# Twelve-sublayer decoder on one core: order of work at the starts, round changes and ends of four sublayers

## The reference, cut to what matters

```python
# layer 0, first attention: 16 heads of 8, a decay on the weights, causal; x += attn(ln(x))
# layer 0, cross-attention (mLSTM, 8 heads of 16), gates from tokens and context:
log_fg = log_sigmoid(f_pre); lf_cs = cumsum(log_fg)
log_d  = lf[t] - lf[s] + i_pre[s], -inf for s > t
m      = max over s of log_d;  d = exp(log_d - m)
out    = ((q k^T) * d) v / (max(|row sum|, exp(-m)) + eps)
# layer 2, first sublayer (Mamba): x_conv = silu(conv(x W_in) + b); B, C, dt from x_conv
h = exp(dt * A) * h + (dt * x_conv) * B;  y = sum over 16 states of h * C
y = (y + x_conv * D) * silu(z);  x += y W_out
# layer 3: a decayed attention over heads (alpha), then sigmoid(layernorm(x)) * wkv
# ("receptance"), then a two-expert MoE with 14 experts
```

## Time and profile before

| | |
|---|---|
| median of 3 runs | 1565.3 us (1560.38, 1565.3, 1567.12) |
| profiled execution | 1562.59 us; its span 1559.7 us, 28295 instructions |
| mean granted TensorE clock | 0.944 |
| mLSTM and MoE of layer 0 | about 157 to 300 us of the span |
| Mamba | about 706 to 977 us |
| layer 3 with the feed-forward ahead of it | about 1207 to 1557 us |

### The profile page before, as it was taken

One profiled execution on the slowest core, in us unless ns is written; L12 is line 12 of the kernel. 1 busy time (PEld: TensorE's weight loads), 2 busy tenths in 40 slices (PEclk: granted clock), 3 DMA queues, 4 the chain that ended last, 5 costly groups with the idle time before them and its releaser, 6 DMA issues. The chain is left out here.

```text
span 1559.7 us, 28295 instructions
## 1 busy us (share of the span) xinstructions
PE 1354.9 (87%) x9646; PEld 885.0 (57%) x9646; DVE 1179.8 (76%) x2532; ACT 879.3 (56%) x2677; POOL 773.8 (50%) x740
## 2 busy tenths in 40 slices
PE   6997887899789998898988988899998678877895
PEld 3554555555567775563333432788887434436784
DVE  7997567789777785465898998777776787887654
ACT  4774342377677773225777775577766244343663
POOL 5667353222655442414988889433336222454553
PEclk9998898999999999999999999999999798878997
DMA  7000000000000000002000000000000400001353
GB/s 312 1 2 1 1 1 1 1 2 2 1 1 2 2 2 0 1 1 97 1 1 1 0 1 1 1 2 1 2 2 6 137 1 1 1 1 53 107 162 99
DMA packets 38494, 39.48 MB, mean 25 GB/s; under 512 B 2128, under 2 KB 35536, under 8 KB 37584
## 3 DMA queue, kind: packets, MB, share of 16 engines
q1 hardware_dynamic: 36304, 33.48, 6.5%
q0 software_dynamic: 2048, 4.20, 0.9%
HBM read 23.52 MB, written 14.16 MB: 24 GB/s over the span
## 5 line engine op out<-in xcount | busy, mean ns | idle before, releaser
L837 POOL TENSOR_TENSOR l_xattn_probs<-l_xattn_probs,l_xattn_recip 128x512 f32<-128x512 f32 x128 | 133.1, 1040 | 220.1 <-DVE l_xattn_recip L776 219.8
L1055 ACT ACTIVATE l_attn_probs<-ps,l_attn_neg_max 128x128 f32<-128x128 f32 x512 | 145.2, 383 | 64.0 <-DVE l_attn_neg_max L1126 62.7
L2786 POOL TENSOR_TENSOR l_mamba_hc<-l_mamba_h,l_mamba_c 128x512 f32<-128x512 f32 x128 | 159.0, 1270 | 0.0
L2707 DVE TENSOR_TENSOR_SCAN l_mamba_h<-ps,l_mamba_dBx 128x512 f32<-128x512 f32 x128 | 152.7, 1213 | 1.8 <-ACT ps L2604 0.7
L2480 PE MATMUL ps<-l_mamba_hc,w_const 128*128 128x512 f32 x256 | 136.3, 638 | 19.2 <-POOL l_mamba_hc L2786 16.5
L771 DVE COPY l_xattn_probsT<-ps 128x512 f32<-128x512 f32 x128 | 88.0, 687 | 69.7 <-PE ps L623 69.7
L246 POOL TENSOR_TENSOR rs<-rs,neg_half 128x4 f32<-128x4 f32 (+1 forms) x32 | 43.4, 1357 | 151.8 <-DVE rs L240 151.7
L722 ACT ACTIVATE l_xattn_probs<-ps,l_xattn_neg_max 128x128 f32<-128x128 f32 x256 | 91.8, 388 | 41.3 <-DVE l_xattn_neg_max L766 41.3
L722 ACT ACTIVATE l_xattn_probs<-l_xattn_biased,l_xattn_neg_max 128x128 f32<-128x128 f32 x256 | 99.3, 391 | 12.2 <-DVE l_xattn_neg_max L766 12.2
L2604 ACT ACTIVATE ps<-l_mamba_th,l_mamba_w_a_bias,l_mamba_w_a_scale 128x508 f32<-128x508 f32 x128 | 97.1, 782 | 13.4 <-DVE l_mamba_h L2707 12.9
L2480 PEld LDWEIGHTS ps<-l_mamba_hc,w_const 128*128 128x128 f32 x256 | 44.8, 194 | 86.7 <-POOL l_mamba_hc L2786 69.3
(11 more groups left out here) (595 smaller groups left out, 3638.3 us busy)
## 6 DMA issues: line engine op xcount, KB each, us to landing
sorted_in<-l_nothing SPq DMA_DIRECT2D x4, 1344.0 KB, 11.5
sorted_out<-l_wide SPq DMA_DIRECT2D x8, 512.0 KB, 3.9
w_early<-in_l_moe SPq DMA_DIRECT2D x1, 3688.0 KB, 12.0
l_large<-sorted_in SPq DMA_DIRECT2D x4, 576.0 KB, 6.3
w_l_xattn<-in_l_xattn SPq DMA_DIRECT2D x1, 2176.0 KB, 18.7
l_large<-sorted_in SPq DMA_DIRECT2D x4, 512.0 KB, 4.4
w_early<-in_l_xattn SPq DMA_DIRECT2D x1, 1890.0 KB, 11.8
sorted_out<-l_wide SPq DMA_DIRECT2D x4, 320.0 KB, 2.6
```

The lines of the kernel that those rows point to most:

```text
L837: nc.gpsimd.tensor_tensor(probs[:, D % 2, n, :, :], probs[:, D % 2, n, :, :], along(recip[:, D % 2, n, :], [P, HALF, P]), ALU.mult).then_i ...
L1055: ins = nc.scalar.activation(probs[:, t % 4, g, :], S_of(t)[:, g * P:(g + 1) * P], ACT.Exp, bias=neg_max[:, t % 2, g:g + 1], accum_out=total)
L2707: nc.vector.tensor_tensor_scan(flat(h[:, t % 2, half, :, :]), G.ps[:, DA_BANK[half], :], flat(dBx[:, t % 2, half, :, :]), 0.0, ALU.mult, A ...
L2786: nc.gpsimd.tensor_tensor(heads4(hc[:, t % 4, half, :]), h[:, t % 2, half, :, :], c_sb[:, t % 3, :, :], ALU.mult).then_inc((hc0_set, hc1_s ...
```

## The change

1. `narrow_attention`, layer 0 only: POOL's `scales` moves from t = 30 to t = 32, behind the last L1182, and its `apply` of 12 blocks (2 per step) becomes 8 blocks after the loop.
2. mLSTM: the last ten instructions of `prepare` move out of the layernorm block to the head of DVE's list (`prepare_split`). The second half of `c_stats` moves behind the rows. ACT does tanh, exp and ln of the forget gate and then tanh of the input gate. `neg_m` is negated before `floor_row`. PE may spread `a_row` before `neg_m` is there, behind 6 instead of 14 `keep_clock` matmuls. POOL's second to fourth `q_pair` wait for the rows.
3. Mamba: `spread_c` goes between the two `add_state` of a step; `x_bc` is taken in halves (n = 10, 11); `x_step`, `steps`, `take_xd`, `tanh` and `step_size` come one to two places earlier; one `tangent_x` moves from n = 10 to n = 9 and DVE's `branch_x(0)` ahead of the second scan of n = 10. At the end DVE's `variances` goes ahead of `gated`, DVE applies 6 blocks, and PE gets 3 and 6 `keep_clock` matmuls.
4. Layer 3: `receptance(0)` goes behind the copy of round 3's tokens, `receptance(1)` ahead of `take_tokens(0)`, and `receive(1)` ahead of `subtract_top(3)`.

```diff
-                if t == DONE:
+                if t == (STEPS if projected else DONE):
                     ahead.scales(pool)
-                if t > DONE and ahead.applied < ahead.first:
+                if not projected and t > DONE and ahead.applied < ahead.first:
                     ahead.apply(pool, nc.gpsimd, 2)
+            if projected:
+                ahead.apply(pool, nc.gpsimd, 8)
...
             nc.vector.tensor_scalar(gain[:], w["gain"], 1.0, None, ALU.add)
+
+        def prepare_split(dve):
+            link = Link(dve, prepared, 2)
             for n in range(2):
...
             score(0)
-            pe.wait_ge(gates_set, 2)
-            keep_clock(14)
-            pe.wait_ge(rows_set, 1)
+            pe.wait_ge(gates_set, 1)
+            keep_clock(6)
             for n, row in enumerate((a_row, neg_m)):
+                if n == 0:
+                    pe.wait_ge(own, 2)
+                else:
+                    pe.wait_ge(rows_set, 1)
...
-            for n, gate in enumerate((gate_f, gate_i)):
-                act.wait_ge(gates_made, n + 1)
-                nc.scalar.activation(gate[:], G.ps[:, G_BANK[1 - n], 0:P], ACT.Tanh, bias=bias15[:, 1 - n:2 - n],
-                                     scale=1.0 / CAP).then_inc(gates_set, 1)
+            act.wait_ge(gates_made, 1)
+            nc.scalar.activation(gate_f[:], G.ps[:, G_BANK[1], 0:P], ACT.Tanh, bias=bias15[:, 1:2], scale=1.0 / CAP).then_inc(gates_set, 1)
             act.wait_ge(gates_set, 1)
-
             nc.scalar.activation(gate_f[:], gate_f[:], ACT.Exp, scale=-CAP).then_inc(gates_set, 1)
-            act.wait_ge(gates_set, 3)
+            act.wait_ge(gates_set, 2)
             nc.scalar.activation(gate_f[:], gate_f[:], ACT.Ln, bias=1.0).then_inc(logs_set, 1)
+            act.wait_ge(gates_made, 2)
+            nc.scalar.activation(gate_i[:], G.ps[:, G_BANK[0], 0:P], ACT.Tanh, bias=bias15[:, 0:1], scale=1.0 / CAP).then_inc(gates_set, 1)
...
-            for half in range(2):
-                c_stats(dve, half)
+            prepare_split(dve)
+            c_stats(dve, 0)
             dve.wait_ge(logs_set, 1)
-            dve.wait_ge(gates_set, 2)
             link(nc.vector.tensor_tensor_scan(cs[:], G.ones[:, 0:P], gate_f[:], 0.0, ALU.mult, ALU.add))
+            dve.wait_ge(gates_set, 3)
             link(nc.vector.scalar_tensor_tensor(a_row[:], gate_i[:], CAP, cs[:], ALU.mult, ALU.add))
             link(nc.vector.tensor_tensor_scan(neg_m[:], zeros[:], a_row[:], NEG, ALU.add, ALU.max))
-            link(nc.vector.tensor_tensor(floor_row[:], cs[:], neg_m[:], ALU.subtract))
-            nc.vector.tensor_scalar(neg_m[:], neg_m[:], -1.0, None, ALU.mult).then_inc(rows_set, 2)
+            nc.vector.tensor_scalar(neg_m[:], neg_m[:], -1.0, None, ALU.mult).then_inc(rows_set, 1)
+            dve.wait_ge(rows_set, 1)
+            nc.vector.tensor_tensor(floor_row[:], cs[:], neg_m[:], ALU.add).then_inc(rows_set, 1)
+            c_stats(dve, 1)
...
-                if q in (1, 2):
-                    c_scales(pool, q - 1)
+                if q == 1:
+                    c_scales(pool, 0)
+                    pool.wait_ge(rows_set, 2)
+                if q == 3:
+                    c_scales(pool, 1)
...
-                if n == 0 and q > 0:
-                    add_state(t - 2, 1)
-                    add_state(t - 1, 0)
                 if n == 3:
                     add_state(t - 2, 0)
-                if n >= 3:
+                if n >= 3 or (n == 0 and q > 0):
                     add_state(t - 2, 1)
-                    add_state(t - 1, 0)
                 if t < LAST:
                     spread_c(t + 1)
+                if n >= 3 or (n == 0 and q > 0):
+                    add_state(t - 1, 0)
...
+                    if n == 10:
+                        x_bc(q + 1, 1)
                     if n == 11:
-                        x_bc(q + 1)
+                        x_bc(q + 1, 0)
+                        x_step(q + 1)
                     if n == 12:
-                        x_step(q + 1)
                         take_high(q + 1, 0)
+                        steps(q + 1, 0)
                     if n == 13:
                         take_high(q + 1, 1)
-                        steps(q + 1, 0)
-                    if n == 14:
                         steps(q + 1, 1)
...
+            keep_clock(nc, G, BC_BANK, 3)
             project_out(NQ - 1, 0)
             project_out(NQ - 1, 1)
+            keep_clock(nc, G, BC_BANK, 6)
...
-                    if n in (7, 10):
-                        tangent_x({7: 1, 10: 0}[n])
-                    if n == 12:
+                    if n in (7, 9):
+                        tangent_x({7: 1, 9: 0}[n])
+                    if n == 11:
                         take_xd(q + 1)
-                    if n in (13, 14):
-                        tanh(q + 1, n - 13)
+                    if n in (12, 13):
+                        tanh(q + 1, n - 12)
...
-                if n == NS - 1 and q + 1 < NQ:
-                    step_size(q + 1, 1)
                 if t < LAST:
                     feed(t + 1)
+                if n == 10 and q + 1 < NQ:
+                    branch_x(q + 1, 0)
                 scan(t, 1)
-                if n == NS - 2 and q + 1 < NQ:
-                    step_size(q + 1, 0)
+                if n in (NS - 3, NS - 2) and q + 1 < NQ:
+                    step_size(q + 1, n - (NS - 3))
...
+            ahead.variances(dve)
             gated(NQ - 1)
-            ahead.variances(dve)
+            ahead.apply(dve, nc.vector, 6)
             add(NQ - 1)
...
                 if q == LAST:
+                    receptance(q - 2)
                     take_tokens(0)
-                    receptance(q - 2)
...
-                if q == LAST - 1:
-                    receptance(0)
...
                 take_attended(q)
+                if q == LAST:
+                    receptance(0)
                 take_q(q)
...
                 if q == LAST:
                     stats(q - 1)
+                    receive(1)
                 subtract_top(q)
                 if q == LAST:
                     below_max(0)
-                    receive(1)
```

More of the change, by code:

```diff
@@ L2499, in _ @@
             keep_clock(nc, G, 4, 6)
-            x_bc(0)
+            x_bc(0, 1)
+            x_bc(0, 0)
             x_step(0)
@@ L2760, in _ @@
                         branch_x(q + 1, 1)
-                    if n == 10:
-                        branch_x(q + 1, 0)
+            ahead.variances(dve)
             gated(NQ - 1)
-            ahead.variances(dve)
+            ahead.apply(dve, nc.vector, 6)
             add(NQ - 1)
```

12 lines of the change are left out of this document (6 added, 6 removed).

## The result

The changed kernel takes 1548.78 us (median of 16 runs, 1542.41 to 1556.08), the kernel before 1563.97 (16 runs, 1554.84 to 1567.12). The ratio is 0.9912, with a 95% interval of 0.9892 to 0.9933: 13.8 us less, between 10.5 and 16.9. (It is a ratio over all runs; the two medians lie 15.2 apart, because the changed kernel's runs fall in two groups, ten up to 1549.2 and six from 1554.5 on.) The forecast was 1553.1, that is 10.7 less, in a range of 1546 to 1562.

What follows compares the result with a forecast made beforehand. No single engine was taken as the limit (TensorE busy 87%, VectorE 76%); the last-ending wait binds each stretch. mLSTM -9.2, Mamba -1.2 and layer 3 -0.3 sum to -10.7, from 1563.85 to 1553.1 us, range 1546 to 1562.

Steps and rivals of the forecast that it cites:

- mLSTM, -9.2: mLSTM: rows and first step come earlier through ACT's order, POOL's wait and early spreading; -9.2 us, between -7 and -10.
- 5.3 forecast: mLSTM up to the rows: the last row leaves DVE at 165.5 instead of 170.8, 5.3 us earlier.
- 3.9 forecast: mLSTM from rows to first step: 3.9 of 8.73 us go, through earlier spreading, the floor's load and faster matmuls.
- Mamba, -1.2: Whole Mamba part: -0.3 us at each of three round changes and -0.3 for the start; between -7 and +7.7.
- at least the 1.22 that DVE waited: Mamba round change: with x_step at n = 11 ahead of spreading B, DVE and POOL wait there at least 1.22 us.
- -0.3 a change: Mamba round changes: nearly the same gap stands at another step, so each of three changes gives -0.3 us.
- rival 1: Mamba gives it back: 1.22 and 1.34 us lost anew at each change, +7.7 in all, time 1561.8; chance 0.18.
- an engine that is busy anyway: Mamba: spreading C one sum earlier brings POOL's read-out forward by 0.9 us, mostly meeting a busy engine.
- Rival 3: Slower: PE idles at n = 11, its clock falls, two steps run at half speed each change; +19.6, 1573.7; chance 0.04.
- 0.97 in Mamba: Mamba round: average granted clock 0.97 in spite of PE waits of 1.58 us, the argument against rival 3.
- Rival 2: Mamba's gaps really vanish: some 2.4 us of DVE's waits go at each change, -7.2, time 1546.9; chance 0.13.
- Layer 3, -0.3: Layer 3: receive(1) begins about 0.9 us sooner, but POOL's products stand there; -0.3, between -1.5 and +0.6.

## Why the prediction was right, and where not

*Start of the block.* Right: +0.45 for the attention's end and some -0.75 for the layernorm block were forecast, +0.56 and -0.77 measured one by one.

*mLSTM, -9.2.* Right in mechanism, and in size against the trace it was taken from. Counted from the block's first matmul, the rows leave 5.0 sooner (5.0 of the 5.3 forecast were meant here, 0.3 being the start), the first step follows them 5.1 later instead of 8.8, 3.6 less (3.9 forecast). The times counted from the span's start are 1.7 to 2.2 late, since the whole program ran 2.0 late from its start. One step was mis-sized: POOL's wait alone is worth 2.6 to 3.4, while I charged the lock with 1.7 in the scan and 0.4 in the negation. And the forecast took from one trace what is not in all: three kernels with the mLSTM as before show the maximum at 0.42 without any wait for it. In one of them POOL's product caught the next instructions instead (floor_row 2.04, the negation 1.72), and the block is 144.3 all the same; in the other two floor_row escaped too (0.29), and the block is 139.9 and 141.5. Over all traces the part saves 7.9 (seven of 143.3 in the mean, six of 135.4), so the size of -9.2 is in part luck of the trace.

*Mamba, -1.2: wrong, it is -7.8, outside the bounds of -7 and +7.7.* What the text named is there: POOL's 2.54 gone, a new gap of DVE and POOL at n = 12, a step size of 1.53 beside POOL. The step that failed is "at least the 1.22 that DVE waited" against the 2.54 saved, which came out at nearly nothing a change. Measured against the kernel before, n = 12 and 13 cost 2.6, above it, and n = 14, 15 and 0 give back 1.3: what I had priced at -0.3 a change costs 1.3, on rival 1's side. The gain comes from what I did not price: n = 1 gives 2.2 and n = 10 gives 0.9. Two terms were missing. One is the clock, 4.0 in all: I read four sums in 3.63 as 0.9 a sum, and they are 0.6 at the upper level. The other is the spreading of C, which I let meet "an engine that is busy anyway": alone it gives 4.8 in the scans and 3.6 in the stage. Rival 3 looked for a clock that falls through the change; the kernel before already had it fall, and the argument "0.97 in Mamba" averaged it away. Rival 2's total for Mamba (-7.2) was right, for another reason.

*Layer 3, -0.3.* Within its bounds by the landmarks, -1.1, but not confirmed: the whole time with this part alone is above the kernel before. DVE's addition no longer meets POOL's product (0.69 instead of 1.66); it runs beside POOL's scalings, and there POOL is the one that takes longer, 0.62.

*The sum.* The forecast of 1553.1 was 4.3 too high. By stages at equal clock, -8.8 - 0.2 - 7.8 - 1.1 = -17.9 would have been too low: the runs show -13.8. So the whole is nearer to the forecast than its parts: mLSTM right, Mamba 6.6 too small, and some 4 lost elsewhere that I had not thought of. That near hit is luck. The stages that the change doesn't touch differ by as much (102.3 or 105.3, 229.0 to 232.2), but whether the rest lies there was not separated.

## What to carry to other kernels

Look at the granted clock in windows of a few us at every place where TensorE waits, not over a round: a duration there that is longer than the same instruction's elsewhere can be a clock that fell, and a reorder that fills the wait, or matmuls that nobody reads, can give more than the wait itself. Here that is 4.0 us in the stage; the whole time of the kernel with such matmuls alone shows no gain (0.9983 to 1.0039). Ahead of a short chain on VectorE, hold GpSimd's long products back by a wait until the chain is done: a wait added there was worth 2.6 us at the first step that needs the chain. When a step is moved earlier, look also at what then stands behind it on the copying engine: B's copy stood behind two others here, and a kernel with it in front, and half of x_step behind the spreading of B, had Mamba 2.5 us shorter.
